# Query, key and value projections of two token tiles as seven block products, and a running sum kept in DRAM

## The chip, the cores and the metric

One core of one Trainium2 chip. The metric is the device time of one execution in microseconds (us). The kernel before has a median of 1268.47 us over three runs (1267.05 to 1268.73). Every number of the trace comes from one profiled execution of 1268.68 us.

## The reference

Two sequences of 512 tokens with 512 channels go through half a feed-forward net (FFN), an attention layer and the same half FFN again. What matters here is the attention layer:

```python
x = x + 0.5 * ffn(layernorm(x))
x = x + attn(layernorm(x))
x = x + 0.5 * ffn(layernorm(x))
# attn: H, HKV, HD = 32, 8, 128; four query heads share one key and value head
q = (x @ Wq.T).reshape(b, s, H, HD); k, v = ... # 8 heads each
q, k = rmsnorm(q, q_norm_w), rmsnorm(k, k_norm_w)
scores = q @ k.T / sqrt(HD) + slopes * (key - query)     # causal
out = softmax(scores) @ v
return out.reshape(b, s, H * HD) @ Wo.T
```

All tensors are float32.

## The kernel before

Every product is done in three matmuls of a rounded float32 format: each operand is split into a high part (rounded by ScalarE, names ending in _h or _hi) and a low part (the rest, by a subtraction on VectorE or GpSimd, names in _l or _lo), and `matmul3` (lines 281 to 286) issues high x high, high x low and low x high. The trace therefore shows nearly all matmuls at lines 284, 285 and 286.

The attention layer runs over 64 units: 8 groups (a key head with its four query heads) times 2 sequences times 4 tiles of 128 tokens. Unit n lies in group n // 8. Its place in the group (0 to 7) is called `at` in the code, its tile number t is `at` modulo 4, and a tile sees (t+1) x 128 keys. The work is software-pipelined, one slot for each unit, and each of the five engines has its own program with a `slot(n)`; engines meet at semaphores only, and each executes its program in order. In slot n TensorE does, in this order (lines 507 to 521): the scores of unit n (12 matmuls of (t+1) x 128 columns); the product of unit n-1's probabilities with its values; the query projection of unit n+4 (4 channel chunks x 3 matmuls of 512 columns, normalized tokens as the stationary side, weights moving); the transposes of unit n+1's rows; the key and value projection of unit n+4 (12 matmuls of 256 columns); the output projection of unit n-1 (12 of 512); the transposes of unit n's probabilities. There are 8 banks of PSUM, taken in rotation; a result waits until its bank was evacuated.

ScalarE's slot (lines 814 to 843): exponentials, copy of the weighted values (oT_h), probabilities times the inverse sum, copy of the query projection to `rows`, qT_h and kT_h, copies of key and value, splits of the next group's weights (at 2 and 3; line 752), high parts of the turned probabilities (probT_h). VectorE's slot (1198 to 1227): reduction of the scores, sum of squares, inverse of the sums, oT_l, in even slots the root steps for two units (`pair_roots`: eleven steps of 10 columns, each waiting for the one before it), qT_l and kT_l, v_l, the running sum x_rows += result, probT_l. GpSimd's slot (1341 to 1356): splits of the output weights (at 1), rows times their inverse roots (line 1339), squares of unit n+4's rows (1333), low parts of the next group's weights. SP's program only issues transfers, in order: the weights of group g+1 when the output weights' splits of group g are done (line 1478), the output weights when the projection weights' splits are done (1486). The running sum x stays on chip for the whole kernel.

The seven-product form is already used in the FFNs (`SEVEN`, lines 52 to 57): a 2x2 block product with sums of blocks on either side.

## Time and profile before

| | us |
|---|---|
| profiled execution | 1268.68 |
| its span | 1267.3 |
| TensorE busy | 1243.2 (98%) |
| VectorE busy | 802.5 (63%) |
| ScalarE busy | 732.8 (58%) |
| GpSimd busy | 523.0 (41%) |
| first slots of group 0, unit 4 (t=0) begins | 315.8 |
| slots of unit 20 to 23 (group 2, at 4 to 7) begin | 512.13, 524.14, 534.90, 547.16 |
| slots of unit 24 to 26 (group 3, at 0 to 2) begin | 561.16, 573.17, 584.08 |
| high part (probT_h, line 807) and low part (probT_l, line 1176) of 512 columns | 0.59 and 0.69 |
| ScalarE's copy of 128 columns (line 771) | 0.27 |
| ScalarE's two casts of 768 columns at 606.19 | 1.58 together |
| a store of 256 KB (y) and a load of 256 KB (x), issue to landing | 2.0 and 5.1 |
| second FFN: its second weights are requested; GpSimd's first work there | 1014.67; 1060.88 for 4.79 |

The slot begins are those of the first score matmul in the chain of waits. TensorE's clock was granted in full (0.97 in the first 50 us, 1.00 after that). The table of busy times says which engine is the fullest; the chain says what the end of the kernel waited for.

### The profile page before, as it was taken

To read this page: it belongs to the slowest core of one execution; us is meant where nothing else is said; L and a number is where in the kernel's file an instruction comes from. 1 tells how busy PE (TensorE), PEld (TensorE's weight loads), DVE (VectorE), ACT (ScalarE), POOL (GpSimd) and SP (SyncE) were. 2 spreads that over 40 slices of the span, in tenths; PEclk is the share of its full clock that TensorE was granted. 3 is DMA by queue.
4 is the path that set the end of the run, shared out by engine and by line. 5 is a ranking of instruction groups with operands and counts; after the bars stand their busy time and mean duration, and the time that the engine had idled before them with its cause. 6 is when DMAs were issued, how large, how long until landed. Compare 5 with 4: busy or idle time off the path is not lost.

```text
span 1267.3 us, 18365 instructions
## 1 busy us (share of the span) xinstructions
PE 1243.2 (98%) x6562; PEld 1059.2 (84%) x6562; DVE 802.5 (63%) x1978; ACT 732.8 (58%) x1738; POOL 523.0 (41%) x412
## 2 busy tenths in 40 slices
PE   6999999999999999999999999999999999999999
PEld 5878888788888888888888888888888878888887
DVE  7966665766665666666566565656666777655554
ACT  4554442367667658567666766666676684544432
POOL 4696551635224224315315314313413242665550
PEclk9999999999999999999999999999999999999999
DMA  6142222101001001001001001001001010121101
GB/s 226 40 153 103 103 101 100 50 1 51 34 1 50 35 1 51 34 1 50 34 1 50 34 1 51 34 1 50 34 1 51 1 50 1 51 80 54 50 17 67
DMA packets 15018, 60.20 MB, mean 47 GB/s; under 512 B 2064, under 2 KB 2736, under 8 KB 12880
## 3 DMA queue, kind: packets, MB, share of 16 engines
q1 hardware_dynamic: 14688, 58.73, 13.3%
q8 instruction: 53, 0.87, 0.3%
q14 instruction: 37, 0.30, 0.1%
q10 hardware_dynamic: 240, 0.30, 0.1%
HBM read 45.91 MB, written 13.11 MB: 47 GB/s over the span
## 4 chain that ended last, share of the span: by engine, by line
PE 93%; DVE 2%; ACT 2%; POOL 1%; issue 1%; DMA 1%; SPq 0%; DVEq 0%; ACTq 0%; POOLq 0%
PE bank L284 28%; PE bank L286 28%; PE bank L285 28%; PE bank L480 5%; PE bank L459 2%; ACT prob L792 1%; PE bank L462 1%; PE bank L312 0%; POOL w_l_early L1264 0%; ACT prob L801 0%; PE bank L300 0%; DVE probT_l L1176 0%; DMA x_rows<-x 0%; DMA raw_early<-ffn_w 0%; PE bank L295 0%
## 5 line engine op out<-in xcount | busy, mean ns | idle before, releaser
L1339 POOL TENSOR_TENSOR rows<-rows,row_root_y 128x640 f32<-128x640 f32 x64 | 80.5, 1258 | 272.2 <-DVE row_root_y L896 272.2
L792 ACT ACTIVATE prob<-prob,neg_top 128x128 f32<-128x128 f32 (+3 forms) x256 | 140.9, 552 | 75.8 <-DVE neg_top L1165 75.2
L1333 POOL TENSOR_TENSOR square<-rows 128x640 f32<-128x640 f32 x64 | 80.3, 1254 | 205.4 <-ACT rows L771 205.4
L807 ACT CAST probT_h<-bank 128x512 fp32r<-128x512 f32 x160 | 84.5, 595 | 136.9 <-PE bank L480 136.9
L801 ACT ACTIVATE prob<-prob,inverse 128x128 f32<-128x128 f32 (+3 forms) x256 | 122.9, 554 | 1.8 <-DVE inverse L1170 1.8
L284 PE MATMUL bank<-w_h_late,xnT_hi 128*128 128x512 f32 (+1 forms) x352 | 121.4, 345 | 0.0
L286 PE MATMUL bank<-w_h_late,xnT_lo 128*128 128x512 f32 (+1 forms) x352 | 118.8, 337 | 0.0
L285 PE MATMUL bank<-w_l_late,xnT_hi 128*128 128x512 f32 (+1 forms) x352 | 118.4, 336 | 0.0
L1264 POOL TENSOR_TENSOR w_l_late<-raw_late,w_h_late 128x512 fp32r<-128x512 f32 (+1 forms) x58 | 87.8, 1533 | 69.6 <-ACT w_h_late L585 69.6
L1176 DVE TENSOR_TENSOR probT_l<-bank,probT_h 128x512 fp32r<-128x512 f32 x160 | 101.6, 686 | 21.8 <-ACT probT_h L807 21.7
L1190 DVE TENSOR_TENSOR x_rows<-bank,x_rows 128x512 f32<-128x512 f32 x64 | 44.2, 691 | 105.1 <-PE bank L286 105.1
L1165 DVE CUSTOM_DVE_ANT_0 prob<-bank,bias 128x128 f32<-128x128 f32 (+3 forms) x256 | 109.8, 486 | 0.0
L1152 DVE SCALAR_TENSOR_TENSOR qT_l<-bank,q_scale,qT_h 128x512 fp32r<-128x512 f32 x64 | 48.0, 751 | 94.9 <-ACT qT_h L780 94.9
L961 DVE SCALAR_TENSOR_TENSOR x_rows<-bank,x_rows 128x512 f32<-128x512 f32 x112 | 75.9, 688 | 46.8 <-PE bank L286 46.8
L284 PE MATMUL bank<-o_h,oT_h 128*128 128x512 f32 x256 | 101.8, 398 | 3.2 <-DVE oT_l L1182 3.2
L285 PE MATMUL bank<-o_l,oT_h 128*128 128x512 f32 x256 | 100.5, 393 | 0.0
L286 PE MATMUL bank<-o_h,oT_l 128*128 128x512 f32 x256 | 100.1, 391 | 0.0
L284 PE MATMUL bank<-kT_h,qT_h 128*128 128x128 f32 (+3 forms) x256 | 86.6, 338 | 1.0 <-DVE qT_l L1152 1.0
L285 PE MATMUL bank<-kT_l,qT_h 128*128 128x128 f32 (+3 forms) x256 | 82.2, 321 | 0.0
L286 PE MATMUL bank<-kT_h,qT_l 128*128 128x128 f32 (+3 forms) x256 | 82.2, 321 | 0.0
L480 PEld LDWEIGHTS bank<-ident,prob 128*128 128x128 f32 x640 | 73.6, 140 | 8.3
L480 PE MATMUL bank<-ident,prob 128*128 128x128 f32 x640 | 80.3, 273 | 0.0
(175 smaller groups left out, 3505.0 us busy)
## 6 DMA issues: line engine op xcount, KB each, us to landing
raw_late<-w_qkv SPq DMA_DIRECT2D x8, 1536.0 KB, 6.3
raw_early<-ffn_w SPq DMA_DIRECT2D x21, 512.0 KB, 4.1
scaled<-raw_early SPq DMA_DIRECT2D x21, 512.0 KB, 2.6
raw_late<-scaled SPq DMA_DIRECT2D x21, 512.0 KB, 3.6
raw_late<-w_o SPq DMA_DIRECT2D x8, 1024.0 KB, 4.8
y<-x_rows SPq DMA_DIRECT2D x8, 256.0 KB, 2.0
x_rows<-x SPq DMA_DIRECT2D x7, 256.0 KB, 5.1
fac_raw_gu<-ffn_fac SPq DMA_DIRECT2D x13, 32.0 KB, 3.4
```

The source lines that it names most:

```text
L284: pe.matmul(bank, lh, rh, start=first, stop=False, skip_group_check=more)
L285: pe.matmul(bank, lh, rl, start=False, stop=False, skip_group_check=more)
L286: return pe.matmul(bank, ll, rh, start=False, stop=last, skip_group_check=more)
L480: last = pe.transpose(bank[:, h * P:(h + 1) * P], prob[:, h, j * P:(j + 1) * P], ident[:, :])
L792: last = act.activation(p, p, ACT.Exp, bias=neg_top[:, h:h + 1], scale=-1.0, accum_out=total[:, h:h + 1])
L801: act.activation(p, p, ACT.Copy, scale=inverse[:, h:h + 1]).then_inc(prob_done, 1)
L807: act.copy(probT_h[:, j, :, :], banks[r.bank][:, :].rearrange("p (h q) -> p h q", h=G)).then_inc(probT_hi_done, 1)
L1165: dve.tensor_tensor_reduce(prob[:, h, 0:keys], banks[r.bank][:, 0:keys], bias[:, h, S - keys:S], -(2.0 ** -g), -MASKED, ALU.add, ALU.min, ...
L1176: dve.tensor_tensor(probT_l[:, j, :, :], banks[r.bank][:, :].rearrange("p (h q) -> p h q", h=G), probT_h[:, j, :, :].bitcast(F32), ALU.sub ...
L1264: return pool.tensor_tensor(lo, raw, hi.bitcast(F32), ALU.subtract)
L1333: pool.tensor_tensor(square[:, n % 2, :, :], row, row, ALU.mult).then_inc(squares_done, 1)
L1339: pool.tensor_tensor(row, row, by, ALU.mult).then_inc(rows_normed, 1)
```

## The change

In groups 2 to 7 the projections of two neighbouring tiles are made together. The tokens are a 2x2 block matrix (tile, half of the channels), the weights one too (half of the channels, left or right 384 of the 768 columns for query, key and value). Seven products of blocks take the place of eight; four of them read sums of token blocks (s1 to s4, formed once, in slots 4 to 7 of group 0, and kept in the room that the running sum had) and four read sums of weight blocks (t1 to t4, formed by GpSimd for each group from 2 on). In groups 0 and 1 the projection is cut in two halves of 384 columns, in place of 512 and 256. Products 1, 6, 7 and 4 add up in PSUM bank 0, ScalarE copies its state out after each of them, and VectorE adds the products 2, 5 and 3 of other banks to these copies. The low part of the values is made by GpSimd in even slots, squares of two units are made at the start of an even slot. The running sum goes to DRAM after the first FFN; each slot loads one tile of it into a ring of two and stores one. The diff, cut to the parts that set the order of the work:

```diff
+PAIRS = B * TB // 2
...
+SEVEN_FROM = 2
+FIRST_PAIRED = SEVEN_FROM * B * TB
+SEVEN_QKV = {1: ("a11", "b11"), 2: ("a12", "b21"), 6: ("s2", "t2"), 5: ("s1", "t1"), 7: ("s3", "t3"), 4: ("a22", "t4"),
+             3: ("s4", "b22")}
...
+        QKV_REST = ({2: ((), ("b11", "b21")), 3: ((), ("b12", "b22"))},
+                    {2: (("t1", "t3", "t2"), ("b11", "b21")), 3: ((), ("t2",)), 4: (("t4",), ("t1", "t3")), 5: ((), ("t4", "b22"))})
+        QKV_WHEN = ({2: ((), ("b11", "b21")), 3: ((), ("b12", "b22"))},
+                    {2: ((), ("b11", "b21")), 3: (("t2",), ()), 4: ((), ("t1", "t3")), 5: (("t4", "b22"), ())})
...
+            def product_qkv(n, m):
+                g, b, t = unit(n)
+                left, block = SEVEN_QKV[m]
...
+                r, bank = result("seven", n, m, bank=None if m in (2, 5) else results["seven", n, 5].bank if m == 3 else 0)
+                w_h, w_l = qkv_place(g, block)
+                for k in range(2):
+                    w = slice(k * HALF, (k + 1) * HALF)
+                    last = matmul3(bank[:, 0:HALF], tokens[k], (w_h[:, w], w_l[:, w]), k == 0 and m in (1, 2, 5), k == 1, True)
                 last.then_inc(full[r.bank], 1)
...
             def slot(n):
+                ahead = n + LEAD
+                first, second = paired(ahead) and n % 2 == 0, paired(ahead) and n % 2 == 1
+                if ahead == FIRST_PAIRED:
+                    rotation[0] = range(1, BANKS)
                 scores(n)
                 if n:
                     weigh_values(n - 1)
-                if n + LEAD < UNITS:
-                    project(n + LEAD, "q")
+                if first:
+                    product_qkv(ahead, 1)
+                    product_qkv(ahead, 2)
+                elif second:
+                    product_qkv(ahead - 1, 5)
+                    product_qkv(ahead - 1, 7)
+                elif ahead < UNITS:
+                    project(ahead, "left")
                 if n + 1 < UNITS:
                     turn_rows(n + 1)
-                if n + LEAD < UNITS:
-                    project(n + LEAD, "kv")
+                if ahead < FIRST_PAIRED:
+                    project(ahead, "right")
                 if n == UNITS - 1:
                     turn_normed(2, 0)
                 if n:
                     project_out(n - 1)
+                if first:
+                    product_qkv(ahead, 6)
+                elif second:
+                    product_qkv(ahead - 1, 4)
+                    product_qkv(ahead - 1, 3)
                 turn_probabilities(n)
+                if ahead == UNITS - 1:
+                    rotation[0] = range(BANKS)
...
+            def split_qkv(g, *blocks):
+                for block in blocks:
+                    if block[0] == "t":
+                        act.wait_ge(qkv_mixed, QKV_MIXES.index((g, block)) + 1)
+                    else:
+                        act.wait_ge(w_in["qkv"], 16 * (g + 1))
...
+                    act.copy(qkv_place(g, block)[0], qkv_raw[block]).then_inc(qkv_hi, 1)
+            def token_sums_round(u):
+                act.wait_ge(x_kept, 16 * B * TB)
+                act.wait_ge(token_sums_done, 4 * (u + 1))
+                act.copy(token_sums[u][1][:, :, :], token_sums[u][0][:, :, :]).then_inc(token_sums_hi, 1)
...
+            def take_sum(n, m):
+                r = results["seven", n, m]
+                act.wait_ge(full[r.bank], r.nth)
+                heads = slice(0, LEFT_HEADS) if m == 1 else slice(LEFT_HEADS, G + 2)
+                act.copy(rows[:, (n + (m == 7)) % LEAD, heads, :],
+                         banks[r.bank][:, 0:HALF].rearrange("p (h d) -> p h d", h=LEFT_HEADS)).then_inc(evac[r.bank], 1)
...
+            def values_hi(n):
+                for u, m in ((n, 3), (n + 1, 5)):
+                    _, b, t = unit(u)
+                    r = results["seven", n, m]
+                    act.wait_ge(evac[r.bank], r.nth)
+                    act.copy(v_h[:, b, t, :], rows[:, u % LEAD, G + 1, :]).then_inc(v_hi_done, 1)
...
+                soon_splits, late_splits = QKV_WHEN[g + 1 >= SEVEN_FROM].get(at, ((), ())) if g < HKV - 1 else ((), ())
+                split_qkv(g + 1, *soon_splits)
...
+                ahead = n + LEAD
+                if ahead < FIRST_PAIRED:
+                    project_left(ahead)
+                elif ahead < UNITS:
+                    take_sum(ahead, 1) if n % 2 == 0 else take_sum(ahead - 1, 7)
+                if n % 2 == 0 and paired(n + 2):
+                    values_hi(n + 2)
                 if n + 1 < UNITS:
                     turn_rows(n + 1)
-                if n + LEAD < UNITS:
-                    project_kv(n + LEAD)
-                elif n < UNITS - 1:
-                    split(1, 0, *(("a11", "a12"), ("a21", "a22"), ("d0", "d1"))[n + LEAD - UNITS])
+                if ahead < FIRST_PAIRED:
+                    project_right(ahead)
+                elif ahead >= UNITS and n < UNITS - 1:
+                    split(1, 0, *(("a11", "a12"), ("a21", "a22"), ("d0", "d1"))[ahead - UNITS])
+                split_qkv(g + 1, *late_splits)
+                if 0 <= n - LEAD < PAIRS:
+                    token_sums_round(n - LEAD)
+                if paired(ahead):
+                    take_sum(ahead, 6) if n % 2 == 0 else take_left(ahead - 1)
...
+            def add_products(n, m):
+                r, taken = results["seven", n, m], results["seven", n, {2: 1, 5: 7, 3: 6}[m]]
+                heads = slice(0, LEFT_HEADS) if m == 2 else slice(LEFT_HEADS, G + 2)
+                row = rows[:, (n + (m == 5)) % LEAD, heads, :]
+                dve.wait_ge(evac[taken.bank], taken.nth)
+                dve.wait_ge(full[r.bank], r.nth)
+                dve.tensor_tensor(row, banks[r.bank][:, 0:HALF].rearrange("p (h d) -> p h d", h=LEFT_HEADS), row,
+                                  ALU.add).then_inc(evac[r.bank], 1)
             def slot(n):
                 late = n + LEAD >= UNITS
                 scores(n)
-                if n + LEAD - 1 < UNITS:
-                    sum_squares(n + LEAD - 1)
+                ahead = n + LEAD
+                if ahead - 1 < FIRST_PAIRED:
+                    sum_squares(ahead - 1)
+                if n % 2 == 0 and paired(n + 2):
+                    sum_squares(n + 2)
+                    sum_squares(n + 3)
...
+                if paired(ahead):
+                    add_products(ahead, 2) if n % 2 == 0 else add_products(ahead - 1, 5)
                 if n + 1 < UNITS:
                     turn_rows(n + 1)
...
                     output_statistics(n - 2)
-                if n + LEAD < UNITS:
-                    values_lo(n + LEAD)
+                if ahead < FIRST_PAIRED:
+                    values_lo(ahead)
                 if n == UNITS - 1:
                     turn_normed(2, 0, (0, 1))
                 elif n:
                     project_out(n - 1)
+                if paired(ahead) and n % 2:
+                    add_products(ahead - 1, 3)
...
+            def mix_qkv(g, *blocks):
+                for block in blocks:
+                    if block == "t1":
+                        pool.wait_ge(w_in["qkv"], 16 * (g + 1))
...
+                    else:
...
+                    left, right = {"t1": ("b12", "b11"), "t2": ("b22", "t1"), "t3": ("b22", "b12"), "t4": ("b21", "t2")}[block]
+                    pool.tensor_tensor(qkv_raw[block], qkv_raw[left], qkv_raw[right], ALU.subtract).then_inc(qkv_mixed, 1)
+            def sum_tokens(u):
...
+                cols = slice(b * S + t * P, b * S + (t + 2) * P)
+                pool.tensor_tensor(whole_pair, xnT_hi[:, :, cols].bitcast(F32), xnT_lo[:, :, cols].bitcast(F32),
+                                   ALU.add).then_inc(whole_pair_done, 1)
...
+                pool.tensor_tensor(s1, a21, a22, ALU.add).then_inc(token_sums_done, 1)
+                pool.tensor_tensor(s3, a11, a21, ALU.subtract).then_inc(token_sums_done, 1)
+                pool.wait_ge(token_sums_done, 4 * u + 1)
+                pool.tensor_tensor(s2, s1, a11, ALU.subtract).then_inc(token_sums_done, 1)
+                pool.wait_ge(token_sums_done, 4 * u + 3)
+                pool.tensor_tensor(s4, a12, s2, ALU.subtract).then_inc(token_sums_done, 1)
+            def token_sums_rest(u):
+                pool.wait_ge(token_sums_hi, u + 1)
+                rest(token_sums[u][2][:, :, :], token_sums[u][0][:, :, :], token_sums[u][1][:, :, :]).then_inc(token_sums_lo, 1)
+            def values_lo(n):
+                for u in (n, n + 1):
+                    _, b, t = unit(u)
+                    pool.wait_ge(v_hi_done, u + 1)
+                    rest(v_l[:, b, t, :], rows[:, u % LEAD, G + 1, :], v_h[:, b, t, :]).then_inc(v_lo_done, 1)
...
                 g, at = divmod(n, B * TB)
                 if at == 1:
                     split_o(g, range(G))
+                ahead = n + LEAD
+                soon, late = QKV_REST[g + 1 >= SEVEN_FROM].get(at, ((), ())) if g < HKV - 1 else ((), ())
+                if n % 2 == 0 and paired(n + 2):
+                    square_rows(n + 2)
+                    square_rows(n + 3)
+                if 0 <= n - LEAD - 1 < PAIRS:
+                    token_sums_rest(n - LEAD - 1)
+                mix_qkv(g + 1, *soon)
+                if n % 2 == 0 and paired(n + 2):
+                    values_lo(n + 2)
                 if n + 2 < UNITS:
                     norm_rows(n + 2)
-                if n + LEAD < UNITS:
-                    square_rows(n + LEAD)
-                elif n < UNITS - 1:
+                if ahead < FIRST_PAIRED:
+                    square_rows(ahead)
+                elif ahead >= UNITS and n < UNITS - 1:
                     if n == UNITS - 3:
                         normalize(2, 0)
-                    split(1, 0, *(("a11", "a12"), ("a21", "a22"), ("d0", "d1"))[n + LEAD - UNITS])
+                    split(1, 0, *(("a11", "a12"), ("a21", "a22"), ("d0", "d1"))[ahead - UNITS])
+                split_qkv(g + 1, *late)
+                if 0 <= n - LEAD < PAIRS:
+                    sum_tokens(n - LEAD)
...
+            def ring_store(n):
+                g, b, t = unit(n)
+                r = results["out", n]
+                sp.wait_ge(evac[r.bank], r.nth)
+                if g < HKV - 1:
+                    sp.dma_start(x_between[b * TB + t], x_ring[:, n % 2, :]).then_inc(ring_out[n % 2], 16)
+            def ring_load(n):
+                g, b, t = unit(n)
+                if n > 1 and unit(n - 2)[0] < HKV - 1:
+                    sp.wait_ge(ring_out[n % 2], 16 * (n // 2))
+                sp.dma_start(x_ring[:, n % 2, :], x_between[b * TB + t]).then_inc(ring_in[n % 2], 16)
...
+            for n in range(UNITS):
+                g, at = divmod(n, B * TB)
+                if at == 1:
+                    if g < HKV - 1:
+                        load_qkv(g + 1)
+                    else:
+                        sp.wait_ge(o_lo, HKV * G)
+                        for kind in KINDS:
+                            load_scaled(0, kind)
+                if at == 6 and g < HKV - 1:
+                    load_o(g + 1)
+                if n:
+                    ring_store(n - 1)
+                if n and n + 1 < UNITS:
+                    ring_load(n + 1)
```

## Rows read from the trace of the kernel before

**Rows 1.** The page: busy time of each engine, and the chain that ended last, by line.
```profile
PE 1243.2 (98%) x6562; PEld 1059.2 (84%) x6562; DVE 802.5 (63%) x1978; ACT 732.8 (58%) x1738; POOL 523.0 (41%) x412
...
PE bank L284 28%; PE bank L286 28%; PE bank L285 28%; PE bank L480 5%; PE bank L459 2%; ACT prob L792 1%; PE bank L462 1%; PE bank L312 0%; POOL w_l_early L1264 0%; ACT prob L801 0%; PE bank L300 0%; DVE probT_l L1176 0%; DMA x_rows<-x 0%; DMA raw_early<-ffn_w 0%; PE bank L295 0%
```

**Rows 2.** Windows: length, then busy us (instructions) of PE, PEld, DVE, ACT, POOL, clock.
```profile
412.20:510.40 98.20, 98.06 (x566) 85.43 (x565) 60.69 (x184) 65.70 (x172) 32.06 (x25) 1.00 0.08 28
```

**Rows 3.** The chain in order of time, one slot: start us, us, what.
```profile
534.90 0.17 PE bank L284
...
536.99 0.23 PE bank L284
...
538.38 0.23 PE bank L284
...
541.11 0.44 PE bank L459 x4
...
541.66 0.12 PE bank L284
...
543.10 0.23 PE bank L284
```

**Rows 4.** The same chain in unit 4's slot.
```profile
324.56 0.23 PE bank L284
...
327.31 0.44 PE bank L480 x4
...
329.24 0.47 PE bank L284
```

**Rows 5.** Groups of instructions: line engine op out<-in xcount, then busy us, mean ns.
```profile
L1333 POOL TENSOR_TENSOR square<-rows 128x640 f32<-128x640 f32 x64 | 80.3, 1254 | 205.4 <-ACT rows L771 205.4
...
L1306 POOL TENSOR_TENSOR mix<-xnT_hi,xnT_lo 128x1024 f32<-128x1024 f32 x4 | 9.6, 2411 | 38.5 <-DVE d_lo L954 38.5
...
L1264 POOL TENSOR_TENSOR fac_down<-fac_raw_down,fac_down 32x256 fp32r<-32x256 f32 x7 | 5.2, 745 | 6.2 <-ACT fac_down L559 6.2
...
L644 ACT CAST mix_h<-mix 128x1024 fp32r<-128x1024 f32 x8 | 8.2, 1049 | 8.4 <-DVE mix L1019 8.4
...
L1264 POOL TENSOR_TENSOR w_l_late<-raw_late,w_h_late 128x768 fp32r<-128x768 f32 x22 | 40.4, 1861 | 0.0
...
L1294 POOL TENSOR_TENSOR mixed<-mixed,raw_late 128x512 f32<-128x512 f32 x6 | 10.0, 1660 | 0.5
...
L752 ACT CAST w_h_late<-raw_late 128x768 fp32r<-128x768 f32 x22 | 17.3, 843 | 0.0
```

**Rows 6.** DMA issues: out<-in queue xcount, KB each, us to landing.
```profile
raw_late<-w_qkv SPq DMA_DIRECT2D x8, 1536.0 KB, 6.3
```

**Rows 7.** GpSimd in order of time, three stretches: start us, us, instruction [idle before].
```profile
18.78 3.76 POOL L1264 TENSOR_TENSOR w_l_early<-raw_early,w_h_early 128x512 fp32r<-128x512 f32 x3
...
579.64 2.55 POOL L1264 TENSOR_TENSOR o_l<-raw_late,o_h 128x512 fp32r<-128x512 f32 x2 [2.72 <-ACT o_h L760]
...
1100.78 3.29 POOL L1264 TENSOR_TENSOR w_l_late<-raw_late,w_h_late 128x512 fp32r<-128x512 f32 x2 [4.50 <-ACT w_h_late L585]
```

**Rows 8.** VectorE in order of time, five stretches.
```profile
21.42 1.14 DVE L887 TENSOR_SCALAR ln_root_m<-mv 128x4 f32<-128x4 f32 x1
...
238.34 0.54 DVE L894 TENSOR_TENSOR ln_root_b<-ln_root_a,ln_root_m 128x4 f32<-128x4 f32 x1
...
528.45 0.69 DVE L1182 TENSOR_TENSOR oT_l<-bank,oT_h 128x512 fp32r<-128x512 f32 x1 [0.29 <-ACT oT_h L812]
...
540.54 0.17 DVE L887 TENSOR_SCALAR row_root_m<-sums 128x10 f32<-128x10 f32 x1
...
542.58 0.17 DVE L896 SCALAR_TENSOR_TENSOR row_root_y<-row_root_b,row_root_y 128x10 f32<-128x10 f32 x1
...
543.02 0.75 DVE L1152 SCALAR_TENSOR_TENSOR qT_l<-bank,q_scale,qT_h 128x512 fp32r<-128x512 f32 x1 [0.27 <-ACT qT_h L780]
...
1100.53 2.39 DVE L1000 TENSOR_TENSOR d_lo<-d,d_hi 128x512 fp32r<-128x512 f32 x2
```

More of the change, by code:

```diff
@@ L21 @@
 G = H // HKV
-QW = G * HD
-QKW = QW + HD
-QKVW = QKW + HD
+QKVW = (G + 2) * HD
+HALF = QKVW // 2
 FI = 1792
@@ L89, in build @@
         w_in = {k: semaphore(f"w_in_{k}") for k in (*KINDS, "qkv", "o")}
+        x_kept = semaphore("x_kept")
+        ring_in, ring_out = ([semaphore(f"ring_{n}{i}") for i in range(2)] for n in ("in", "out"))
         w_out = {k: semaphore(f"w_out_{k}") for k in KINDS}
@@ L760, in split_o, with project_left @@
                     act.copy(o_h[:, k, :], o_raw[:, k, :]).then_inc(o_hi, 1)
[L762 to L763 removed]
+            def project_left(n):
+                r = results["left", n]
                 act.wait_ge(full[r.bank], r.nth)
[L765 to L767 removed]
+                act.copy(rows[:, n % LEAD, 0:LEFT_HEADS, :],
+                         banks[r.bank][:, 0:HALF].rearrange("p (h d) -> p h d", h=LEFT_HEADS)).then_inc(evac[r.bank], 1)
@@ new lines, in take_sum, with take_left @@
+            def take_sum(n, m):
[3 more added lines that the diff above has]
+                act.copy(rows[:, (n + (m == 7)) % LEAD, heads, :],
+                         banks[r.bank][:, 0:HALF].rearrange("p (h d) -> p h d", h=LEFT_HEADS)).then_inc(evac[r.bank], 1)
+            def take_left(n):
+                r = results["seven", n, 4]
+                act.wait_ge(full[r.bank], r.nth)
+                act.copy(rows[:, (n + 1) % LEAD, 0:LEFT_HEADS, :],
+                         banks[r.bank][:, 0:HALF].rearrange("p (h d) -> p h d", h=LEFT_HEADS)).then_inc(evac[r.bank], 1)
```

232 lines of the change are left out of this document (147 added, 85 removed).

## The prediction

> **What bounds the kernel now.** I read the busy times and the chain first. TensorE works through the whole span at full clock, and the chain lies on its three matmul lines [rows 1]. The attention stage repeats every 98.2 us (eight slots, one per query tile); in one such period TensorE is busy for all but 0.14 us, ScalarE for 65.7, VectorE 60.7, GpSimd 32.1 [rows 2]. So a TensorE microsecond removed there is gained as long as no other chain comes due earlier than it did. The chain in order of time gives the cadence of each matmul shape, which "mean ns" (overlapping durations) does not: twelve 384-column matmuls take 536.99-534.90 = 2.09 us (0.174 each), twelve of 512 columns 541.11-538.38 = 2.73, twelve of 256 columns 543.10-541.66 = 1.44 [rows 3].
>
> I call S the first score matmul of a slot, t its tile number (0 to 3) and "at" its place in the group (0 to 7).
>
> **TensorE's work.** A pair of tiles costs 2 x (2.73+1.44) = 8.34 us now. Seven products of 2x3 matmuls with 384 columns are 42 x 0.174 = 7.31. Gain 1.03 a pair. Groups 2 to 7 are done so, 24 pairs: **-24.8 us**. Groups 0 and 1 (24 matmuls of 384 for 12+12) come out even: 4.18 against 4.17 a tile. Nothing else of TensorE's changes in number. But even slots now hold three products (3.1 us) and odd ones four (4.2), and, more important, only two of them (2.1 us) stand ahead of the output projection where 4.17 stood: it comes due 2.1 us earlier in every slot.
>
> **Token sums, slots 4 to 7 of group 0.** ScalarE's order is: copies of the projection, then the rounding of the token sums, then the copies of the turned probabilities of this slot. The rounding waits for GpSimd's sums of the same slot, and these stand behind GpSimd's square, which waits for the same projection's copy. Nothing hides this. Slot 4 is in the trace; K = 324.56 is the end of its projections [rows 4]. After K: copy of two heads, 0.37 as I estimate (128 columns take 0.27, table of times); square 1.25; whole pair, 1024 columns, 2.41; four sums of 256 columns, for which I take 0.745 (256 columns on 32 partitions) = 3.0; ScalarE's rounding of 1024 columns 1.05 [rows 5]. That is K+8.2; probT_h 0.59 and probT_l 0.69 (table of times) on top: K+9.6. TensorE wants it at 329.24 = K+4.7. Stall 4.9. In slot 5 the same instant comes due at K+2.75+0.87+2.09 = K+5.7: 3.9. Behind this VectorE's and ScalarE's softmax chain is 5.1 late while TensorE is 3.9 late, so in slot 6 the copies of the projection start some 1.3 us after it ended, and the roots hold GpSimd 0.5 longer: 9.6+1.8-6.8 = 4.6. In slot 7 the lag is 2.2: 6.0. Sum **+19.4 us**; without the lags 15.5, with sums at 0.9 and longer lags 22. From slot 8 on the four-tile slots' own slack takes up the rest.
>
> **Weight sums against the roots, slot at=2.** The weights of the next group are requested when the o_l splits end, 582.19, and need 6.3 us: 588.5, which is S+4.4 to 4.7 of slot 2 (S = 584.08, table of times) [rows 6, 7]. Then GpSimd makes t1, t3 and t2 of 768 columns without a pause, 1.86 each by the nearest row (512-column mixes of 1.66 would scale to 2.4) [rows 5]. VectorE's eleven small root steps of that slot want to start at about S+5.7, 540.54 in the like slot that starts at 534.90, and now end at S+7.9 [rows 8]. What happens where both meet can be read elsewhere. A four-column root step issued at 21.42 took 1.14 instead of 0.17 and ended when GpSimd's subtraction ended (18.78+3.76 = 22.54) [rows 7, 8]. And two VectorE steps with two SBUF inputs, issued 0.25 before a pair of GpSimd subtractions, took 2.39 where 1.3 is usual and the subtractions 3.29 where 2.5 is: they take turns [rows 7, 8]. In turns, the first root step waits to S+6.7, the second to 8.6, the third to 10.5; two halves of v_l (0.46 each) hold two more; the last six take 0.2 each: roots at S+13.1. Behind them on VectorE stand the sum of product 2 (0.5) and the next tile's qT_l and kT_l (0.95, [rows 8]): S+14.6. TensorE has the next scores due at 2.09+1.38+2.09+0.55+2.75+1.04+1.31 = S+11.2. Stall 3.4, in groups 2 to 6; in group 1, whose slot is still the old one (12.3 us long, no v_l on GpSimd), 1.1. Sum **+18.1 us**. The ends: nothing, if the small steps slip in one behind the other, and 26, if a mix takes 2.3 and the weights land 1 us later. I take 18.1 because a step of four columns was held for the whole subtraction.
> The Trainium skill (SBUF — State Buffer, Who interferes with whom) has this as a rule: a VectorE instruction with two SBUF inputs, or one in a 2-port mode, and a GpSimd instruction that reads SBUF exclude each other for the whole instruction. The trace agrees where both have two inputs, yet not everywhere: of eleven root steps that ran beside GpSimd's tensor_scalar at 237 to 240 us, ten took their usual 0.16 to 0.19 and only one 0.54 [rows 8]. By the rule the sum is mine; by those rows it would be 18 us less.
>
> **The output projection that comes due earlier.** It needs oT_l. t=1: due at 1.43+0.3+0.68+2.09+0.55 = S+5.05; oT_l ends at 528.45+0.69 = 529.14, S+5.0 [rows 8]. No slack is left, and at=5 puts two casts of 768 columns (0.84 [rows 5], 1.58 for two) ahead of the exponentials, which have 1.1 us of idle time before them: 0.4 late, six times; at=1 0.1, six times. **+3.0 us**. t=2: due S+6.1, oT_l at S+5.75 even with two square sums ahead of it. t=0: due 6.7, ready 5.5. t=3: due 7.5, ready 6.4 to 7.1. Bounds 0 and 8.
>
> **Costed at nothing.** ScalarE: four copies of 384 for two each of 512, 128 and 128. VectorE: three sums of 384 (0.55 each) a pair for two v_l of 0.28, 65 us of 94 a period. GpSimd: four mixes, two more splits, v_l: about 47 us of 94. Bank 0's waits: product 6 is due at S+8.9 (t=2), the copy that frees it ends at S+7.7; product 4 at S+7.9 (at=1) and 7.5; 0.4 of cover, lost if ScalarE is later. Seven banks in rotation for eight: the oldest is always evacuated. The running sum: 8+56 stores and 64 loads of 256 KB, 33.5 MB; SP issues the load for tile n+1 behind the store of n-1, some 5 us (2.0 for a store, up to 5.1 for a load, table of times) before the slot after next, which has 7 us more. SP waits for the weights' room at at=1 and 6, both passed within the slot. At the end SP is held in the ring until slot 63, so the second FFN's next weights are requested near 1042 and not at 1014.67; GpSimd gets to them after 1065.7 (table of times).
>
> **Sum.** The profiled execution took 1268.68 (span 1267.3 and 1.4 around it), 0.2 over the median of 1268.47. 1268.7 - 24.8 + 19.4 + 18.1 + 3.0 = **1284**.
>
> **Rivals.**
> (A) No turns: small steps get their port between GpSimd's reads, as the rows at 237 us speak for; 1284.4-18.1 = 1266. Not slower. It decides by itself: if roots end before S+9.7 there is no stall. Against it: the held four-column step.
> (B) Both waits covered (GpSimd's 256-column sums and ScalarE's order cheaper than read): 1247. Against it: the order of both programs is explicit.
> (C) The token wait is small, the turns are real: 1265.
> (D) Slower still: oT_l late in all t=1 and t=2 slots. 24 slots, 0.05 and 0.35 of slack; 1 us later on ScalarE or VectorE costs 12 x 0.95 + 12 x 0.65 = 19: 1303. It decides from 0.1 us at t=1. For it: new ScalarE and VectorE work in each slot; against: little of it stands ahead of oT_l.
> (E) The products are not cheaper (384 columns slower here than in the scores): 24.8 us more, 1309; its cadence is in the trace, so hardly.
>
> **Chances.** Main 0.52, its own range 1274 to 1294; A 0.14; B 0.12; C 0.07; D 0.13; E 0.02. The range takes all but B and the upper half of D and E: 1262 to 1298. A measurement tells 0.2% (2.5 us) from no change. Faster by more (below 1265.9): B and half of A and C, 0.22; within: the other half and a little of the main case, 0.12; slower 0.66.
>
> **What would show it.** In the profile after: matmuls of 384 columns at 0.174; TensorE idle for probT_l for 4 to 6 us in each of four slots between about 327 and 385 us, ScalarE there waiting for GpSimd; later periods of about 94 + 3.4 + 0.5 us; root steps of over 1 us beside GpSimd's mixes, 3 to 5 in one slot of eight, and TensorE waiting for qT_l behind them; short waits for oT_l in t=1 slots. Wrong, if a period is 94 us or less (no turns), if those four slots are not longer than 13 us each (no token wait), or if waits for oT_l or bank 0 come in most slots (D).

## The result, and the profile after

The changed kernel takes 1290.18 us (median of 4 runs, 1288.86 to 1292.91) where the kernel before took 1267.99 beside it: 1.0181 times as long, 95% interval 1.0165 to 1.0196. That is 22 us slower; 1284 was forecast, in a range of 1262 to 1298. The profiled execution has a span of 1288.4 us against 1267.3.

The page of the changed kernel first: busy times, then the chain that ended last by engine, then the DMA lines of the running sum.

```profile
PE 1234.4 (96%) x6418; PEld 1073.1 (83%) x6418; DVE 848.0 (66%) x2002; ACT 757.7 (59%) x1760; POOL 650.5 (50%) x526
...
PE 74%; ACT 9%; DVE 6%; POOL 5%; issue 4%; DMA 1%; SPq 0%; ACTq 0%; POOLq 0%; DVEq 0%
...
x_ring<-x_between SPq DMA_DIRECT2D x64, 256.0 KB, 2.6
x_between<-x_ring SPq DMA_DIRECT2D x56, 256.0 KB, 2.0
```

TensorE has 144 matmuls fewer than in [rows 1] and is busy 8.8 us less, yet the span grew by 21.1: TensorE stood for 54.0 us where it had stood for 24.1. A fifth of the chain (20%) now runs through ScalarE, VectorE and GpSimd, where they had 5% before. The running sum's 64 loads and 56 stores are there, and no wait of TensorE leads to one.

Where TensorE stood is read from its waits, here in the stretch 322 to 400 us and then in 480 to 960 us (engine, what it computes, line, what released it: us in all, times, longest):

```profile
PE bank L346 <- DVE probT_l L1324: 15.2, 4, 4.9
```
```profile
PE bank L346 <- POOL o_l L1432: 6.9, 10, 1.1
PE bank L346 <- DVE kT_l L1305: 4.1, 4, 1.6
PE bank L346 <- DVE oT_l L1330: 1.3, 5, 0.3
PE bank L346 <- DVE qT_l L1300: 0.6, 1, 0.6
```

The first line is the predicted wait for the token sums. In the second block the lines on kT_l, qT_l and oT_l are the predicted ones. The line on o_l, the low part of the output weights, is the largest, and the prediction has no such term.

The rows of TensorE's weight loads (PEld) show short waits that those of the matmuls leave out. From 480 to 960 us, first the kernel before, then the changed one (two lines), then the kernel with all four moves:

```profile
PEld bank L284 <- POOL o_l L1264: 1.4, 5, 0.3
```
```profile
PEld bank L346 <- POOL o_l L1432: 11.2, 10, 1.5
...
PEld bank L346 <- DVE oT_l L1330: 3.6, 10, 0.5
```
```profile
PEld bank L346 <- DVE oT_l L1330: 2.1, 10, 0.2
```

Slot by slot (from one first score matmul to the next; groups are numbered from 0; "all four off" is the experiment further down in which these waits are gone):

| slot | before | after | all four off |
|---|---|---|---|
| token sums, slots 5 to 8 of the attention | 10.77, 12.25, 14.00, 12.01 | 17.99, 17.91, 18.66, 17.43 | 10.84, 12.32, 14.05, 12.09 |
| group 1, at=2 | 12.26 | 13.08 | 12.32 |
| groups 2 to 6, at=0 | 12.01 | 11.02 | 11.03 |
| at=1 (2 to 7) | 10.91 | 12.97 to 13.00 | 11.03 |
| at=2 | 12.26 | 12.29, 12.38, 12.26, 13.11, 12.12 | 11.25 |
| at=3 | 14.00 | 14.07 | 14.07 |
| at=4, 5, 6, 7 | 12.01, 10.76, 12.26, 14.00 | 11.02, 11.35, 11.25, 14.07 | 11.03, 11.05, 11.24, 14.07 |

**The token sums.** GpSimd, ScalarE and TensorE in order of time, in the first of the four slots (start us, us, instruction, [idle before, who ended it]):

```profile
323.60 1.25 POOL L1557 TENSOR_TENSOR square<-rows 128x640 f32<-128x640 f32 x1 [0.43 <-ACT rows L887]
324.81 2.39 POOL L1519 TENSOR_TENSOR xn<-xnT_hi,xnT_lo 128x1024 f32<-128x1024 f32 x1
```
```profile
330.26 1.05 ACT L866 CAST sum_h<-sum 128x1024 fp32r<-128x1024 f32 x1 [6.58 <-POOL sum L1529]
```
```profile
332.66 0.77 PE L346 MATMUL bank<-probT_h,v_h 128*128 128x512 f32 x1 [4.92 <-DVE probT_l L1324]
```

ScalarE does nothing for 6.58 us, because its cast of the sums stands ahead of probT_h in its program; TensorE waits 4.92 behind it. What follows was not foreseen. Windows of the same stretch (columns as in [rows 2]; the number behind the five engines is the granted clock):

```profile
328.00:330.00 2.00, 0.00 (x0) 0.00 (x0) 0.00 (x0) 0.00 (x0) 1.92 (x4) 1.00 0.28 67
330.00:332.00 2.00, 0.00 (x0) 0.00 (x0) 0.17 (x1) 1.53 (x2) 0.79 (x2) 0.73 0.31 107
332.00:334.00 2.00, 1.34 (x3) 1.16 (x4) 2.00 (x10) 1.11 (x5) 2.00 (x2) 0.50 0.00 0
334.00:336.00 2.00, 2.00 (x7) 1.92 (x6) 1.32 (x3) 2.00 (x7) 0.96 (x1) 0.50 0.00 0
336.00:338.00 2.00, 2.00 (x9) 1.96 (x9) 0.17 (x1) 1.05 (x3) 0.00 (x0) 0.56 0.00 0
338.00:344.00 6.00, 6.00 (x37) 5.44 (x35) 1.70 (x4) 1.82 (x5) 2.84 (x2) 1.00 0.02 4
```

TensorE stood idle from 327.74 to 332.66. The granted clock fell to 0.50 (the 1.2 GHz level) while it stood, and stayed at that level for some 5 us after it had begun again; the six us from 332 to 338 hold 19 matmuls, the six from 338 on 37. A lower clock costs nothing while TensorE stands, so what it cost is read from the stretches behind the four waits, to the end of each slot:

```profile
332.66:344.06 11.40, 11.40 (x52) 10.52 (x53) 4.59 (x15) 5.99 (x18) 5.21 (x4) 0.78 0.01 2
350.24:361.97 11.73, 11.73 (x59) 10.77 (x60) 7.68 (x27) 6.66 (x18) 5.69 (x4) 0.85 0.06 25
367.73:380.63 12.90, 12.90 (x66) 11.59 (x67) 6.93 (x17) 7.62 (x19) 6.00 (x5) 0.87 0.01 1
385.91:398.06 12.15, 12.15 (x57) 10.68 (x58) 7.11 (x29) 5.84 (x20) 3.61 (x3) 0.87 0.00 0
```

At full clock they would be about 0.22 x 11.40 + 0.15 x 11.73 + 0.13 x 12.90 + 0.13 x 12.15 = 7.5 us shorter, an estimate. 15.2 of waits and these 7.5 are 22.7; the four slots grew by 22.96.

**The output weights, at=1.** ScalarE, GpSimd and TensorE in order of time:

```profile
500.88 1.13 ACT L874 CAST o_h<-raw_late 128x512 fp32r<-128x512 f32 x2
```
```profile
501.57 2.50 POOL L1432 TENSOR_TENSOR o_l<-raw_late,o_h 128x512 fp32r<-128x512 f32 x2 [2.72 <-ACT o_h L874]
```
```profile
502.88 0.50 PE L346 MATMUL bank<-o_h,oT_h 128*128 128x512 f32 x1 [1.11 <-POOL o_l L1432]
504.12 0.50 PE L346 MATMUL bank<-o_h,oT_h 128*128 128x512 f32 x1 [0.28 <-POOL o_l L1432]
```

Heads 2 and 3 of the output weights are cast in ScalarE's part of slot at=1 behind the probabilities, and GpSimd makes their low parts after that. The same pair on GpSimd is in [rows 7] at 579.64: there it ended at 582.19, S+9.0 of its slot, and the output projection, behind 4.17 us of projections, waited only 0.28 us for it (the 1.4 in five slots above). Now it wants them 2.1 us earlier, and the weight loads wait 11.2 us in five slots, 2.2 in each.

**The turns, at=2.** GpSimd, then VectorE:

```profile
510.77 1.86 POOL L1507 TENSOR_TENSOR xn<-raw_late 128x768 f32<-128x768 f32 x1 [0.39 <-DMA raw_late<-w_qkv]
512.71 1.85 POOL L1507 TENSOR_TENSOR raw_late<-raw_late 128x768 f32<-128x768 f32 x1
514.51 1.85 POOL L1507 TENSOR_TENSOR xn<-raw_late,xn 128x768 f32<-128x768 f32 x1
```
```profile
513.08 0.69 DVE L1330 TENSOR_TENSOR oT_l<-bank,oT_h 128x512 fp32r<-128x512 f32 x1
513.69 0.89 DVE L1035 TENSOR_SCALAR row_root_m<-sums 128x10 f32<-128x10 f32 x1
514.62 1.77 DVE L1037 TENSOR_SCALAR row_root_y<-row_root_m 128x10 int32<-128x10 int32 x1
516.43 0.38 DVE L1040 SCALAR_TENSOR_TENSOR row_root_a<-row_root_y 128x10 f32<-128x10 f32 x1
```

The second mix ends at 514.56 and the step m at 514.58; the third ends at 516.36 and y ends at 516.39. The turns are as forecast, but there are two long ones and not three. oT_l, which has one input in PSUM and one in SBUF, took its usual 0.69 beside the second mix. The weights came at 510.7, S+3.0 of this slot (S = 507.80), and not at S+4.7: their transfer starts in slot at=1, which is 2 us longer by the wait for o_l.

### The profile page after: what moved, and what is told of

The parts are those of the page before. It is cut to its first block, busy times and chain, and to the rows that moved or that the text cites. A ratio compares the mean times of both kernels' runs of the same rounds, so it can differ in the third digit from the quotient of the medians.

```text
span 1288.4 us, 18592 instructions
## 1 busy us (share of the span) xinstructions
PE 1234.4 (96%) x6418; PEld 1073.1 (83%) x6418; DVE 848.0 (66%) x2002; ACT 757.7 (59%) x1760; POOL 650.5 (50%) x526
## 4 chain that ended last, share of the span: by engine, by line
PE 74%; ACT 9%; DVE 6%; POOL 5%; issue 4%; DMA 1%; SPq 0%; ACTq 0%; POOLq 0%; DVEq 0%
PE bank L346 23%; PE bank L348 23%; PE bank L347 22%; ACT prob L932 4%; PE bank L564 3%; ACT prob L941 2%; DVE probT_l L1324 1%; PE bank L543 1%; POOL o_l L1432 1%; ACT oT_h L952 1%; POOL xn L1519 1%; ACT probT_h L947 1%; ACT w_h_late L861 1%; ACT rows L896 1%; POOL sum_l L1432 1%
## 5 line engine op out<-in xcount | busy, mean ns | idle before, releaser
L346 PE MATMUL bank<-o_h,oT_h 128*128 128x512 f32 x256 | 106.8, 417 | 13.0 <-POOL o_l L1432 8.3
L1349 DVE TENSOR_TENSOR rows<-bank,rows 128x384 f32<-128x384 f32 x72 | 40.0, 556 | 80.8 <-ACT rows L896 47.4
L346 PE MATMUL bank<-probT_h,v_h 128*128 128x512 f32 x160 | 66.1, 413 | 16.9 <-DVE probT_l L1324 15.9
L346 PEld LDWEIGHTS bank<-o_h,oT_h 128*128 128x128 f32 x256 | 48.1, 188 | 29.8 <-POOL o_l L1432 14.0
L1432 POOL TENSOR_TENSOR w_l_early<-raw_early,w_h_early 128x512 fp32r<-128x512 f32 x37 | 49.6, 1359 | 41.9 <-ACT w_h_early L689 41.8
L1432 POOL TENSOR_TENSOR v_l<-rows,v_h 128x128 fp32r<-128x128 f32 x48 | 21.2, 464 | 90.2 <-ACT v_h L912 90.2
```

The source lines that it names most:

```text
L346: pe.matmul(bank, lh, rh, start=first, stop=False, skip_group_check=more)
L1432: return pool.tensor_tensor(lo, raw, hi.bitcast(F32), ALU.subtract)
```

## The experiments

The kernel before was timed beside each. The first four are single moves of the changed kernel, the fifth is all of them, and the last four are the changed kernel with work added.

**The token sums' cast a slot later.** ScalarE casts the sums of pair u one slot after GpSimd made them, and GpSimd's rest is moved one slot later too (not shown).

```
-                if 0 <= n - LEAD < PAIRS:
-                    token_sums_round(n - LEAD)
+                if 0 <= n - LEAD - 1 < PAIRS:
+                    token_sums_round(n - LEAD - 1)
```

> ScalarE rounds the token sums one slot later, GpSimd takes their low part one slot later. Theory (order of ScalarE's program makes it wait for GpSimd, which holds the turned probabilities; TensorE then idles 15.2 us in four waits, and its clock falls to the lower level for a while behind each): slots 5 to 8 return from 17.99, 17.91, 18.66 and 17.43 to about 10.8, 12.3, 14.1 and 12.1 us, no wait for probT_l there, clock 1.00; time 23 us less, about 1267. Rival (GpSimd itself is too full in these slots, 10.2 us of work in 10.8): the waits move to other tiles and 5 to 10 us of the 23 remain, about 1275.

Measured: 1268.09 us, 1.0005 of before (0.9995 to 1.0014), span 1267.1. The four slots are 10.84, 12.33, 14.04 and 12.09 and the clock is 0.999 over the span. The whole excess of the stage, clock and all, hung on this one place in ScalarE's order. GpSimd's sums themselves, 5.4 us a slot, cost nothing.

**The output weights cast a slot earlier.** Heads 0 and 1 in slot at=0 ahead of the copies of the turned probabilities, 2 and 3 behind them.

```
-                if at == 1:
-                    split_o(g, (2, 3))
+                if at == 0:
+                    split_o(g, (0, 1))
 ...
                 if at == 0:
-                    split_o(g, (0, 1))
+                    split_o(g, (2, 3))
```

> ScalarE makes all four high parts of the output weights in slot at=0, two of them before the copies of the turned probabilities, in place of two in slot 0 and two after the probabilities of slot at=1. Theory (the output projection comes due 2.1 us earlier and now meets the low parts of the output weights): the six at=1 slots of groups 2 to 7 go from 12.97 to 10.9 us, no wait for o_l; the next group's weights are then requested 4 us earlier, the three mixes reach the roots with one left, and the at=2 slots keep 0.5 to 1.1 us; about 13 us less, 1277. Rival (oT_l is the late one, behind the exponentials): the slots fall to 12 us at best, 1284.

Measured: 1277.42 us, 1.0081 of before (1.0066 to 1.0096). The at=1 slots are 11.03 to 11.06, the wait for o_l is gone, and the at=2 slots are 11.86. Slot 1 of group 0 is 11.79 for 10.88, and at=1 of group 1 11.49 for 10.93, the price of the move. In the trace the six at=1 slots give back 11.6, the at=2 slots 3.6, and the price is 1.5; the median gained 12.8. The 11.6 is the term that the prediction lacks.

**The mixes behind the scale of the rows, at=2.** GpSimd's three mixes stand behind norm_rows, so that VectorE's root steps are over when they run; ScalarE's cast of t2 goes to the end of slot at=3 (not shown).

```
-                mix_qkv(g + 1, *soon)
+                if at != 2:
+                    mix_qkv(g + 1, *soon)
 ...
                     norm_rows(n + 2)
+                if at == 2:
+                    mix_qkv(g + 1, *soon)
```

> In slot at=2 GpSimd makes t1, t3, t2 after the normalized rows (so after VectorE's roots) and ScalarE casts t2 at the end of slot 3. Theory (VectorE's root steps and GpSimd's two-input subtractions take turns): all root steps 0.17 us, at=2 slots of groups 2 to 6 from 12.29, 12.38, 12.26, 13.11, 12.12 to 11.25, that of group 1 from 13.08 to 12.3, time 6.8 us less, 1283. Rival (the slot is late because VectorE has more of its own to do before qT_l: two square sums, a product's sum): the root steps get short but the slots stay above 12 us, 1288 to 1290.

Measured: 1283.73 us, 1.0129 of before (1.0112 to 1.0146). The at=2 slots are 11.24, the one of group 1 is 12.28. The turns cost 6.5 us.

**t4 cast a slot earlier**, so that one cast of 768 columns and not two stands ahead of slot at=5's exponentials.

```
-                    {... 4: ((), ("t1", "t3")), 5: (("t4", "b22"), ())})
+                    {... 4: ((), ("t1", "t3", "t4")), 5: (("b22",), ())})
```

> ScalarE casts t4 at the end of slot at=4, with t1 and t3, and only b22 at the start of slot at=5. Theory (two casts of 768 columns ahead of the exponentials outlast ScalarE's idle time and make oT_l late for the output projection): at=5 slots of groups 1 to 6 from 11.35 to 10.85, 3 us less in all, 1287. Rival (three casts in slot 4 delay the copies behind them, as much is lost there): no change, 1290.

Measured: 1288.9 us, 1.0169 of before (1.0154 to 1.0184). The at=5 slots went from 11.35 to 11.05 to 11.09, which is 1.6 us in six slots; the median gained 1.3, inside what a measurement tells from nothing. The expected 3 was too much.

**All four moves.**

> The four single moves put together: the cast of the token sums a slot later, heads 2 and 3 of the output weights cast in slot at=0, the at=2 mix behind the scale of the rows, and t4 cast in slot at=4. If the four waits are separate and each was taken away whole by its own move, the savings add: 1290.2 - 22.1 - 12.8 - 6.5 - 1.3 = 1247.5, 1.5% under the kernel before; that is also the old rival B, which priced the change with both waits covered. A rival: the moves overlap, because the output weights moved alone had already shortened the at=2 slots by 0.4 each (the 2.5 us that the move of the mix would take again), and a shorter at=1 slot lets the transfer of the weights land later against slot at=2; then 1250 to 1253. If taking the waits away lets something else end last (the running sum's trip through DRAM among it), 1256 or more, and a slot of a kind that is now at 11.0 to 11.3 is longer.

Measured: 1249.63 us (1248.24 to 1250.44), 0.9853 of before (0.9838 to 0.9868): 1.5% faster than the kernel before, 3.1% than the changed one. The page:

```profile
PE 1221.7 (98%) x6418; PEld 1068.4 (86%) x6418; DVE 830.7 (67%) x2002; ACT 756.9 (61%) x1760; POOL 649.9 (52%) x526
...
PE 93%; DVE 2%; ACT 2%; POOL 1%; issue 1%; DMA 1%; SPq 0%; DVEq 0%; ACTq 0%; POOLq 0%
```

The chain is TensorE's again, and from 480 to 960 us TensorE's matmuls show no wait (its weight loads show the 2.1 us for oT_l above). The result lies at the rival: added whole, the savings make 1247.5; the overlap of 2.5 between the output weights and the turns makes 1250.

**TensorE kept busy in the token wait.** Matmuls without use ahead of the wait for probT_l, first in all four slots (20, 14, 14, 14), then without the last.

```
                 r, bank = result("values", n)
+                for _ in range({4: 20, 5: 14, 6: 14, 7: 14}.get(n, 0)):
+                    pe.matmul(bank[:, :], v_h[:, b, 0, :], xnT_hi[:, 0, 0:S], start=True, stop=True)
```

> The changed kernel, with matmuls of no use to it (20, 14, 14 and 14 of 512 columns, into the bank that the values product then starts anew) ahead of the wait for probT_l in the second to fifth slot of the token sums' stage. The result is unchanged by them. The chain of ScalarE and GpSimd still makes TensorE wait the same 15.2 us in all, so if the other 7.7 of the 22.9 is the clock that falls after TensorE sat idle, the clock stays at 0.97 or more in these slots, and the kernel is 6 to 8 us faster: 1283. If the 7.7 is other waits (VectorE and ScalarE late behind the same chain), it is the same, 1290, or slower by what the added matmuls exceed the waits.

Measured: 1290.8 us, 1.0184 of before (1.0167 to 1.0201). The four slots are 15.66, 16.35, 18.29 and 23.24. The windows of the first slot's wait, and the chain at the fourth's:

```profile
330.00:332.00 2.00, 1.88 (x9) 1.22 (x7) 0.56 (x1) 1.41 (x2) 0.99 (x1) 1.00 0.14 52
332.00:334.00 2.00, 1.81 (x9) 1.68 (x10) 2.00 (x10) 1.49 (x6) 2.00 (x2) 1.00 0.04 8
```
```profile
381.88 0.70 DVE probT_l L1326
...
382.72 6.02 PE bank L576 x14
```

In the first slot the clock stays at 1.00 and the slot is 2.33 us shorter with the same chain behind it: ScalarE's cast of the sums comes at 4.2 us into the slot in both. In the fourth the added matmuls came behind the wait (their bank is freed by the same late step), and did harm. So the clock did what the first expectation says in three slots, and the time did not: 1290.8 where 1283 was expected.

> The changed kernel with the useless matmuls (20, 14 and 14) in the second to fourth slot of the stage alone. In the fifth the four of before stood behind the wait, not ahead of it: their bank comes free by the same late VectorE step, TensorE sat idle 5.2 us all the same and then took 6.0 us for the 14 at the lower clock, and the slot grew from 17.4 to 23.2. Without them the fifth slot should be at 17 to 18 again and the three others keep what they gained (2.3, 1.6 and 0.4): 1290.2 - 4.3 = 1286. If the gain of the three slots was only moved into the fifth (the chain of ScalarE and GpSimd ends when it ends), the fifth is at 21 and the kernel at 1290.

Measured: 1288.51 us, 1.0163 of before (1.0149 to 1.0177). The slots are 15.68, 16.36, 18.32 and 20.08. Windows, one for about each slot:

```profile
325.00:341.00 16.00, 15.68 (x89) 13.71 (x87) 5.93 (x17) 7.33 (x20) 10.84 (x9) 1.00 0.11 34
341.00:358.00 17.00, 16.45 (x91) 14.61 (x90) 8.71 (x29) 8.57 (x21) 9.87 (x9) 1.00 0.26 94
358.00:376.00 18.00, 17.22 (x93) 14.88 (x92) 7.77 (x18) 9.91 (x22) 9.96 (x9) 1.00 0.09 30
376.00:395.00 19.00, 13.77 (x64) 12.09 (x63) 7.91 (x29) 8.23 (x23) 8.80 (x8) 0.82 0.08 28
```

The result lies between the two expectations, nearer to the second. The clock holds in three slots, which gain 2.3, 1.5 and 0.3; the fourth gives back 2.65. Its wait is 5.2 where it had been 3.7, and the clock falls there. So with the clock kept the waits grow: what TensorE loses at half clock it would in part have lost waiting for the same chain. The first matmul behind the wait starts 6.55, 6.11, 6.95 and 6.76 us into its slot, where it had been 6.59, 6.18, 5.76 and 5.28. The stage gains 1.55 us, the median 1.7, and neither is beyond what this can tell from nothing: without fillers the four slots took 71.6 to 73.0 us in six profiled executions, with the three fillers 70.4. The spread is in the first slot (17.12 to 17.99) and in the fourth, which takes 17.3 to 17.4 at a clock of 0.90 in three of the executions and 18.6 to 18.8 at 0.82 in the other three, after the same wait of 3.7. Against those three the fourth slot with fillers gave back only some 1.4.

**The turns by themselves.** Four operations of 512 columns on GpSimd, their result unused, behind the squares of slot at=6 in groups 2 to 6, where the change has no collision; once with two inputs in SBUF, once with one.

```
+                if at == 6 and 1 < g < HKV - 1:
+                    for k in range(4):
 ...
+                        pool.tensor_tensor(xn_flat[:, 1536:2048], xn_flat[:, 0:512], xn_flat[:, 256:768], ALU.add).then_inc(probed, 1)
```
```
+                        pool.tensor_scalar(xn_flat[:, 1536:2048], xn_flat[:, 0:512], 1.0, None, ALU.mult).then_inc(probed, 1)
```

> The changed kernel, with four additions of 512 columns by GpSimd (two inputs in SBUF, the result unused) behind the squares of slot at=6 of groups 2 to 6, where nothing of the change collides with the root steps of VectorE. If VectorE's steps on operands in SBUF wait out the instruction that GpSimd has running, then the root steps m, y, a and b of these slots take 0.5 to 1.3 each in place of 0.16, and the slot grows from 11.25 by 1 to 3 us, part of it because the scale of the rows on GpSimd also comes up to 5 us later: 1294 to 1302. If GpSimd's operations alone do it, by making GpSimd's own later work late, the steps stay at 0.16 and the slots grow all the same.

Measured: 1292.3 us, 1.0193 of before (1.0173 to 1.0214); the at=6 slots are 11.84, 11.58, 11.57, 11.57 and 11.58 instead of 11.25, 1.9 us in all. That is 0.3 to 0.6 a slot where 1 to 3 was expected. The whole time is not told apart from the changed kernel's; the verdict rests on these slots and the steps in them. GpSimd, then VectorE:

```profile
659.73 5.43 POOL L1579 TENSOR_TENSOR xn<-xn 128x512 f32<-128x512 f32 x4
```
```profile
663.07 0.73 DVE L1036 TENSOR_SCALAR row_root_m<-sums 128x10 f32<-128x10 f32 x1
663.84 0.17 DVE L1038 TENSOR_SCALAR row_root_y<-row_root_m 128x10 int32<-128x10 int32 x1
664.04 1.15 DVE L1041 SCALAR_TENSOR_TENSOR row_root_a<-row_root_y 128x10 f32<-128x10 f32 x1
```

> The same as with two inputs, but the four operations of GpSimd have one input in SBUF and a constant (the rows at 237 of before, where root steps of VectorE ran in 0.16 beside such an operation with a conversion). If one input leaves VectorE free, the root steps of slot at=6 stay at 0.16 to 0.2, and only GpSimd's own lateness is left: the slot grows by at most 1 us where the other kernel's grows by more. If any GpSimd operation on SBUF holds VectorE's steps, the steps lengthen as with two inputs.

Measured: 1292.08 us, 1.0194 of before (1.0172 to 1.0216), which is again not told apart from the changed kernel; the at=6 slots are 11.24 or 11.25 throughout. In the profiled run one slot of group 5 (at=3, 15.68 for 14.07) is 1.6 longer than its likes. Its window says why: TensorE is busy in all of it, at a granted clock of 0.89.

```profile
814.86:830.54 15.68, 15.68 (x78) 13.80 (x79) 8.94 (x20) 8.71 (x20) 7.29 (x5) 0.89 0.16 51
```

TensorE had waited 2.09 us for kT_l just before. The same stands in the profile with three fillers (15.66 at 0.89, behind a wait of 1.85), so it is not the added work of this kernel. Nor does it follow every such wait: behind one of 2.13, in the profile of the kernel with t4 cast earlier, the clock stayed at 1.00 and the slot at 14.03. The same views as with two inputs:

```profile
656.67 6.21 POOL L1579 TENSOR_SCALAR xn<-xn 128x512 f32<-128x512 f32 x4
```
```profile
660.00 0.45 DVE L1036 TENSOR_SCALAR row_root_m<-sums 128x10 f32<-128x10 f32 x1
660.49 0.17 DVE L1038 TENSOR_SCALAR row_root_y<-row_root_m 128x10 int32<-128x10 int32 x1
660.70 0.17 DVE L1041 SCALAR_TENSOR_TENSOR row_root_a<-row_root_y 128x10 f32<-128x10 f32 x1
...
661.52 0.51 DVE L1043 TENSOR_TENSOR row_root_b<-row_root_a,row_root_m 128x10 f32<-128x10 f32 x1
```

Beside operations with two inputs (1.3 us each) a step that meets one waits until it is over, up to 1.15. Beside operations with one input (1.49 each, so longer) five root steps in a row take 0.17, and the one that meets the start of the next takes 0.5. The two kernels differ in the number of inputs and in the operation (an addition, a product with a constant), so which of these two does it stays open. The steps m and y, which have one input themselves, wait all the same beside two inputs (0.73 here, 1.77 in the changed kernel). The Trainium skill (SBUF — State Buffer, Who interferes with whom) has a GpSimd instruction that reads SBUF and a VectorE instruction with two SBUF inputs, or in a 2-port mode, which tensor_scalar can enter, exclude each other for the whole instruction. The runs bear that out beside GpSimd's two inputs; beside its one input, a and b (two inputs each) took 0.17, with at most 0.35 on top, and there they don't.

## Why the prediction came out, and what in it was wrong

The total is 6 us off, with errors of up to 12 us in its terms that nearly cancel: the turns were put 11.4 too high, and a wait worth 11.7 was missed. That these two meet is luck, and so is the period of eight slots, forecast at about 97.9 and measured at 97.9 to 98.9: its parts are others. Each term beside what the runs gave for it:

| term | forecast | measured | from |
|---|---|---|---|
| seven products for eight | -24.8 | -20.6 | slots 12 to 59, 589.20 before and 568.60 with all four off |
| token sums | +19.4 | +22.7 | 71.99 - 49.30 (those four slots with all four off); 22.1 in the median |
| turns, at=2 | +18.1 | +6.7 | groups 1 to 6 against all four off; 6.5 in the median |
| oT_l, at=5 | +2.4 | +1.7 | 6 x 0.29; 1.3 in the median |
| output weights, at=1 | (0.6, for oT_l) | +11.7 | 6 x 1.95; 12.8 in the median, with 3.6 from at=2 |
| sum | +15.7 | +22.2 | span: +21.1 |

The last 1.1 lies outside these slots: the attention begins at 270.17 in the changed kernel's profile and at 271.83 in that of before, its other slots are 0.9 longer, and the rest is 0.4 shorter. The early begin is no effect of the change: in the profiles of the changed kernel and its variants it lies between 269.56 and 271.78.

**The products.** The cadence of 0.174 was right within some 0.01: a product of six takes 1.05 to 1.06 (527.84, 528.90, 529.95 with all four off). The even slots lost 0.98 to 1.01 for 1.04. The odd ones were to stay as they were and are 0.07 to 0.29 longer even with all four off. At t=1 most of that is the predicted wait for oT_l, in a size that the prediction had wrong:

```profile
524.98 0.19 PEld L346 LDWEIGHTS bank<-o_h,oT_h 128*128 128x128 f32 x1 [0.21 <-DVE oT_l L1330]
```

The prediction has the output projection due at S+5.05 and oT_l ready at S+5.0. It took S from the chain (524.14); the first score matmul of that slot starts at 523.90 in the timeline, and so oT_l ends at S+5.24, in the kernel before as in this one. So TensorE waits for it some 0.2 us at at=1 and, in the changed kernel, 0.5 at at=5, where 0.1 and 0.4 were forecast; 0.2 stays at at=5 with all four off. The -20.6 holds this 0.2 in twelve slots, some 2.5 us; without it the products are near -23.

**The token sums.** The mechanism, its place and the first slot's size were right: TensorE was to want probT_l at K+4.7 and get it at K+9.6, a wait of 4.9; it waited 4.92. (That it fits to 0.02 is partly luck: the terms that it lists add up to K+9.3, a wait of 4.6. In the trace the projections end at 322.95, and GpSimd's square starts 0.65 behind that, where 0.37 was allowed.) The four waits are 4.92, 3.82, 2.74 and 3.75, 15.2 in all, where the prediction without its lags has 4.9, 3.9, 2.8 and 3.8. The lags by which 19.4 was reached are not there in that form; in their place stands the clock, which the prediction takes as 1.00 throughout. By the fillers the two are not separate sums: with the clock kept, the slots gave back some of it in longer waits. The clean figure for the clock is the 2.33 us of the first slot, after a wait of 4.9; the estimate from the granted clock is 0.22 x 11.40 = 2.5 there.

**The turns.** Right in kind: the held steps end when GpSimd's instructions do. The size was off by the time at which the weights land. The prediction took the request from the slots of before (o_l's splits end at S+9.0 of slot at=1) and the length of slot at=1 as unchanged. That slot grew by 2 us behind the same o_l, so the mixes ran at S+3.0 to S+8.6, and two root steps met them, not three. (Even with the forecast landing, the terms listed add up to S+12.6 for the end of the roots, not S+13.1.) With the output weights moved and the weights requested earlier still, the at=2 excess fell further, to 0.6 a slot.

**What was missed.** The prediction says that the output projection comes due 2.1 us earlier in every slot, and asks only for oT_l. It has a second input, the low parts of the weights, and at=1 is their first use in a group. The pair of o_l at 579.64 to 582.19 [rows 7] was quoted for another purpose; beside it stands this row of the kernel before, the fourth head's first matmul of the same slot, which the prediction did not look up:

```profile
582.24 0.50 PE L284 MATMUL bank<-o_h,oT_h 128*128 128x512 f32 x1
```

It starts 0.05 us after the low part that it needs, S+9.1, and its weight load had waited 0.28 for it. So this chain had no slack already, and the 2.1 us of products that now stand behind the output projection were to lengthen the slot whole: 2.1 in each of six slots, some 12.5 us. It was 11.7.

**The rivals.** A and C fell with the turns and the token wait in the trace. B's condition is what the kernel with all four moves meets, and its price was near: 1249.6 for 1247. D's condition (oT_l late in all t=1 and t=2 slots) is met in the t=1 slots only, and small: the weight loads waited 3.6 us for oT_l in 480 us. E fell with the cadence.

## What to carry to other kernels

When a block of work moves ahead of its consumers' old due time, list every operand of the consumer and when each is ready in the slot where that is latest, not only the one that was critical before. When an engine in the middle of a chain casts what another engine makes, put the cast where its input is already there; here one slot later was worth 22 us. And GpSimd's operations with two inputs go where VectorE has only work with an input in PSUM, or behind its small steps. Count slack from one clock: a slot begin from the chain and an end from the timeline differed by 0.24 us here, which was all the slack there was.

## What the runs showed of the hardware

- After 4.9 us in which TensorE stood, the granted clock was 0.50 (1.2 GHz of 2.4) for about 5 us of its next work. With TensorE kept busy through the wait the slot ran at 1.00 and took 15.66, where it took 17.12 to 17.99 in the six profiles without fillers.
- Shorter waits did it too, and not every time. Behind waits of 2.09 and 1.85 us the clock fell (0.89 over the next slot, 1.6 us longer), behind one of 2.13 it stayed at 1.00. After one and the same wait of 3.7 the slot's clock was 0.90 in three executions and 0.82 in three others.
- VectorE's steps on 10 columns, with one SBUF input as with two, were held to the end of a GpSimd tensor_tensor (up to 1.8 for 0.17), but ran at 0.17 beside a GpSimd tensor_scalar of one input, with one step in each such instruction at 0.45 to 0.52. VectorE's reductions of 640 columns beside either took 0.81, which is their usual time, and oT_l, with one input in PSUM, its usual 0.69 beside a tensor_tensor.
- 16.8 MB of loads and 14.7 MB of stores of the running sum, 2.6 and 2.0 us each, left no wait on TensorE.
